# Local attention: the reciprocal of the denominators inside the queries' rotation, and the value products in another order

## The chip, the cores and the metric

The kernel runs on one core of a Trainium2 chip. The metric is the device time of one execution in microseconds (us); the median of three runs is given. TensorE (PE in the profile) does the matmuls and transposes, VectorE (DVE) and ScalarE (ACT) the elementwise work and what is read out of PSUM, GpSimd (POOL) elementwise work between SBUF tensors, and SyncE (SP) issues the transfers.

## The reference, cut to what matters

The whole is a macaron block: half of a two-layer local-attention network, a global attention, and half of the same local-attention network again, over x of 4 x 1024 tokens with 128 channels. The change touches only the local attention, which therefore runs four times (two passes of two layers). Per layer:

```python
q = l2norm(q) * qs;  k = l2norm(k) * ksc          # 8 heads of 64
q, k = rotary_xpos(q, k)                           # x * cos + rotate_half(x) * sin
sim = einsum('bhwid,bhwjd->bhwij', bq, bk)         # 64 queries see their own and the previous block of 64 keys
sim = where((i < j) | (i > j + WINDOW) | (j == -1), -max, sim)
attn = softmax(sim, axis=-1)
out = einsum('bhwij,bhwjd->bhwid', attn, bv)
x = x + out @ wo
```

The softmax is done in pieces: the maximum, the exponentials with their sum (the denominator), one reciprocal of eight sums per row, and a multiplication by it.

## The kernel before, in words

A layer has 32 tiles of 128 tokens. `local_attention_pass` writes the program of each engine out by hand, in order: a `body(i, k)` for the first 28 tiles of a layer, then a written-out end (`attention_end`) in which the last four tiles are woven with the start of the layer's MLP. There are four such stages, so 112 bodies. Engines wait for each other by counting semaphores only; each engine takes its own list strictly as it is written. In the body of tile k the steps belong to different tiles, up to four ahead:

- **PE**: key projection of tile k+4 (L199); eight transposes of tile k's probabilities (L252, the first four into one PSUM bank, the rest into another); query projection of k+4 (L204); value projection of k+3 (L210); the value products of tile k (L268); the scores of k+2 (L239); eight transposes of k+3's rotated and scaled queries and keys (L221); the output projection of k (L279).
- **VectorE**: sums of squares of k+3 (L382); one half of the transposed probabilities of k out of PSUM (`dve_probsT`, L419); the clipped norm of k+3 in four small steps (`dve_clip_norm`, L389, L391, L394, L398); the rotation of k+4's keys and then of its queries (`dve_rotate`, three multiplications each: L374, L375, L376); the reciprocal of k+1 (`dve_inv`, L414); the masked scores and maxima of k+2 (`dve_max`, L404 and eight times L406); the residual of k (L424).
- **GpSimd**: scale the rotated queries and keys of k+3 by their norms (`gp_rotary_scale`, L294, waits for `norm_ready` from L398); multiply the probabilities of k+1 by the reciprocals (`gp_normalise`, L301, waits for `inv_done` from L414); add the two parts of the rotation of k+4 (`gp_rotary_sum`, L288, waits for `q_rotated` from the queries' L376).
- **ScalarE**: exponentials of k+1, slots 2 and 3 (L333); the logarithm and inverse root for the norm of k+3 (L322, L325); the other half of the transposed probabilities (L354); squares of k+4's queries (L308); exponentials of k+1, slots 4 to 7, after which `exp_done` is signalled; copies of the values (L318) and heads (L359); squares of the keys (L313); the first exponential of k+2, the copies of transposed queries and keys (L341, L349, and every fourth tile L348), the second exponential.

`dve_inv` waits for `exp_done` of its tile and for `probs_ready` of two tiles before. The value products of a tile are 16 matmuls in the text: four pairs of heads, two heads of a pair (e), two windows. Head e of a pair uses output partitions 64e to 64e+63, so one half of the columns of the array; window 0 reads `v_first`, window 1 reads `v_second`. The last of the 16 is preceded by the waits of the next scores (`pe_await_scores`).

Of the kernel before, what the change touches and what calls it, by code (L numbers as in the profile page):

```python
# [19 lines left out]
TILE = 128  # L20
# [4 lines left out]
HEADS, DH = 8, 64  # L25
# [20 lines left out]
def tile_of(i, k):  # L46

    return i + k // BATCH_TILES, k % BATCH_TILES
# [93 lines left out]
def local_attention_pass(nc, C, K, W, probs, probsT, z_in, z_out, x, first):  # L142
# [3 lines left out]
    with ExitStack() as ctx:  # L146
        def sb(name, shape, dt=F32):
            return ctx.enter_context(nc.sbuf_tensor(C.own(name), shape, dt))
# [14 lines left out]
        v_second = sb("v_second", [P, 4, INNER])  # L163
        v_first = sb("v_first", [P, 4, INNER])
# [10 lines left out]
        ps = ctx.enter_context(nc.psum_tensor(C.own("ps_attn"), [P, 8, 512], F32))  # L175
        QB, KB, VB, SB0, B5, B6, OB = 0, 1, 2, 3, 5, 6, 7

        def waiting(eng):
            def wait(name, i, k, lag=0, per=1, less=0):

                eng.wait_ge(C[name], i * (BATCH_TILES * per) + (C.at[name] + per * (k + 1 - lag) - less))
            return wait
# [6 lines left out]
        def wait_values(eng, i, k):  # L189

            name = f"v_in{k % 4}"
            eng.wait_ge(C[name], i * 64 + (C.at[name] + 32 * (k // 4 + 1)))
# [33 lines left out]
        def pe_await_scores(pe, wait, i, k):  # L226
            wait("qT_ready", i, k)
            wait("kT_ready", i, k)
            wait("max_done", i, k, 1, HEADS)
# [25 lines left out]
        def pe_values(pe, wait, i, k, scores_next):  # L255
            wait("p5_read", i, k)
            wait("p6_read", i, k)
            wait_values(pe, i, k)
            wait("heads_ready", i, k, 1)
            for pair in range(4):  # L260
                for e in range(2):
                    cols = slice((2 * pair + e) * DH, (2 * pair + e + 1) * DH)
                    out = ps[64 * e:64 * e + 64, OB, pair * TILE:(pair + 1) * TILE]
                    for window, v in ((0, v_first), (1, v_second)):
                        if scores_next and (pair, e, window) == (3, 1, 1):
                            pe_await_scores(pe, wait, *tile_of(i, k + 2))
                        queries = slice(WINDOW * window, WINDOW * (window + 1))
                        last = nc.tensor.matmul(out[:, queries], v[:, k % 4, cols], probsT[:, 4 * e + pair, queries], start=True,  # L268
                                                stop=True, skip_group_check=True)
            last.then_inc(C["av_done"], 1)  # L270
# [88 lines left out]
            nc.scalar.copy(oT[:, :, :], ps[:, OB, :].rearrange("p (a t) -> p a t", t=TILE)).then_inc(C["heads_ready"], 1)  # L359


        def dve_rotate(dve, wait, which, i, k):

            if which:
                wait("k_done", i, k)
                wait("qk_ready", i, k, 2)
            else:
                wait("q_squared", i, k)
            h0 = which * HEADS
            x = ps[:, QB + which, :].rearrange("p (h d) -> p h d", d=DH)  # L370
            table = W["rotary"][:, i // B, k, :, :]
            cos = table[:, which, :].unsqueeze(1).to_broadcast([P, HEADS, DH])
            sin = table[:, 2 + which, :].unsqueeze(1).to_broadcast([P, HEADS, DH])
            nc.vector.tensor_tensor(rot_a[:, k % 2, h0:h0 + HEADS, :], x, cos, ALU.mult)  # L374
            nc.vector.tensor_tensor(rot_b[:, k % 2, h0:h0 + HEADS, 0:32], x[:, :, 32:64], sin[:, :, 0:32], ALU.mult)  # L375
            nc.vector.tensor_tensor(rot_b[:, k % 2, h0:h0 + HEADS, 32:64], x[:, :, 0:32], sin[:, :, 32:64], ALU.mult  # L376
                                    ).then_inc(C["k_rotated" if which else "q_rotated"], 1)

        def dve_ssq(dve, wait, i, k):
            wait("k_squared", i, k)  # L380
            wait("norm_log", i, k, 2)
            nc.vector.reduce_sum(ssq[:, k % 2, :], sq[:, :].rearrange("p (h d) -> p h d", d=DH), AX_X  # L382
                                 ).then_inc(C["ssq_done"], 1)

        def dve_clip_norm(dve, wait, i, k):

            r, n = inorm[:, k % 2, :], newton[:, k % 2, :]
            wait("norm_inv", i, k)
            nc.vector.tensor_tensor(n, r, r, ALU.mult).then_inc(C["newton"], 1)  # L389
            wait("newton", i, k, 0, 2, 1)  # L390
            nc.vector.scalar_tensor_tensor(out=n, in0=n, scalar=-0.5, in1=ssq[:, k % 2, :], op0=ALU.mult, op1=ALU.mult  # L391
                                           ).then_inc(C["newton"], 1)
            wait("newton", i, k, 0, 2)
            nc.vector.scalar_tensor_tensor(out=n, in0=n, scalar=1.5, in1=r, op0=ALU.add, op1=ALU.mult  # L394
                                           ).then_inc(C["newton_done"], 1)
            wait("newton_done", i, k)
            wait("qk_ready", i, k, 2)
            nc.vector.tensor_scalar(cnorm[:, k % 2, :], n, NORM_MOST, None, ALU.min).then_inc(C["norm_ready"], 1)  # L398

        def dve_max(dve, wait, i, k):  # L400
            wait("p6_turned", i, k, 2)
            wait("exp_done", i, k, 2)
            wait("scores_done", i, k)
            nc.vector.memset(slack[:, :], 0.0)  # L404
            for slot in range(HEADS):
                nc.vector.tensor_tensor_reduce(probs[:, k % 2, slot, :],  # L406
                                               ps[:, SB0 + slot // 4, (slot % 4) * SPAN:(slot % 4 + 1) * SPAN],
                                               K["masks"][:, 0 if k == 0 else 1, :], -1.0, MOST, ALU.add, ALU.min,
                                               negmax[:, k % 2, slot:slot + 1]).then_inc(C["max_done"], 1)

        def dve_inv(dve, wait, i, k):
            wait("exp_done", i, k)
            wait("probs_ready", i, k, 2)
            nc.vector.reciprocal(iden[:, k % 2, :], den[:, k % 2, :]).then_inc(C["inv_done"], 1)  # L414

        def dve_probsT(dve, wait, i, k):
            wait("p6_turned", i, k)
            wait("av_done", i, k, 1)
            nc.vector.tensor_copy(probsT[:, 4:8, :], ps[:, B6, :].rearrange("p (a t) -> p a t", t=TILE)).then_inc(C["p6_read"], 1)  # L419

        def dve_residual(dve, wait, i, k):
            wait("wo_done", i, k)
            c = tile_column(i % B, k)
            nc.vector.tensor_tensor(z_out[:, bass.ds(c, TILE)], ps[:, VB, 0:TILE], z_in[:, bass.ds(c, TILE)], ALU.add  # L424
                                    ).then_inc(C["z_done"], 1)
# [232 lines left out]
        def ahead(i, k, n):  # L658

            return 0 <= BATCH_TILES * (i % B) + k + n < TILES  # L660
# [5 lines left out]
        def _(pe):  # L666
# [23 lines left out]
            def attention_end(layer):  # L690
                pe_centre(pe, wait, layer, 0)
                pe_transpose_probs(pe, wait, *t(layer, 28), True)
                pe_project_values(pe, wait, *t(layer, 31))
                pe_values(pe, wait, *t(layer, 28), True)
                pe_scores(pe, *t(layer, 30))
                pe_transpose_qk(pe, wait, *t(layer, 31))
# [4 lines left out]
                pe_transpose_probs(pe, wait, *t(layer, 29), True)  # L701
                pe_var(pe, wait, layer, 1)
                pe_values(pe, wait, *t(layer, 29), True)
                pe_scores(pe, *t(layer, 31))
                pe_centre(pe, wait, layer, 2)
# [372 lines left out]
        def _(dve):  # L1078
            wait = waiting(dve)
            nc.vector.memset(kT[:, :, 0:WINDOW], 0.0).then_inc(C["pass_set"], 1)  # L1080

            def body(i, k):
                if ahead(i, k, 3):
                    dve_ssq(dve, wait, *tile_of(i, k + 3))
                if ahead(i, k, 0):
                    dve_probsT(dve, wait, i, k)
                if ahead(i, k, 3):
                    dve_clip_norm(dve, wait, *tile_of(i, k + 3))
                if ahead(i, k, 4):
                    dve_rotate(dve, wait, 1, *tile_of(i, k + 4))  # L1090
                    dve_rotate(dve, wait, 0, *tile_of(i, k + 4))
                if ahead(i, k, 1):
                    dve_inv(dve, wait, *tile_of(i, k + 1))
                if ahead(i, k, 2):
                    dve_max(dve, wait, *tile_of(i, k + 2))
                if ahead(i, k, 0):
                    dve_residual(dve, wait, i, k)
# [67 lines left out]
            for tile in range(WOVEN):  # L1165
                body(*t(0, tile))
# [40 lines left out]
            for tile in range(WOVEN):  # L1207
                body(*t(1, tile))
# [1582 lines left out]
```

## Time and profile before

| | |
|---|---|
| median of the runs | 1967.95 us (1967.82 to 1968.98) |
| the profiled execution | 1970.34 us, span 1968.4 us |
| busy share of the span | PE 96%, DVE 84%, ACT 76%, POOL 47% |
| one body in the steady part of a stage | 7.58 us |

A line of the profile names the engine, the line of the kernel, the operation, output and input, how many, how long, and, in brackets, how long the engine was idle before and what ended that. PEld is TensorE's loading of weights, which runs beside its matmuls. The ends of matmuls are modelled and consecutive ones overlap, so TensorE's pace is read from where its instructions start. The share of PE is of the whole program; the change sits in the four stages of local attention.

### The profile page before, as it was taken

The numbers are of one execution on the slowest core, as the hardware profiler recorded it, in microseconds if no ns is written. First come the engines' busy times: TensorE is split into PE (matmuls) and PEld (weight loads), VectorE is DVE, ScalarE is ACT, GpSimd is POOL, SyncE is SP. The second block draws the span as 40 slices with busy tenths as digits, with TensorE's granted clock in tenths as the row PEclk, the third lists the DMA queues.
The fourth block names the chain that finished last, engine by engine and source line by source line (L and its number), as shares of the span: only waits on it lengthen the run. The fifth ranks groups of instructions, "written<-read, shape, count | busy, mean of one in ns | idle before, by whom it ended". The sixth has DMA issues, their size and how long they took to land. (4 is left out here: it accounts for less than half of the span.)

```text
span 1968.4 us, 61233 instructions
## 1 busy us (share of the span) xinstructions
PE 1891.7 (96%) x22590; PEld 1117.6 (57%) x22590; DVE 1649.2 (84%) x5474; ACT 1502.9 (76%) x4121; POOL 915.5 (47%) x548
## 2 busy tenths in 40 slices
PE   7999999999999989999999998899999999999998
PEld 3777763577775343443443367436777645777753
DVE  6899975899995678999999769769999659999955
ACT  5899994799997353777777754469999848999963
POOL 2778760488882040000000046338887406888800
PEclk9999999999999986999999999999999999999999
DMA  6112120112121040111111000002222201121201
GB/s 188 44 44 48 44 67 6 33 45 49 44 66 23 6 154 27 41 41 42 42 42 42 20 5 2 2 20 49 45 47 45 58 6 42 43 49 44 67 16 43
DMA packets 76138, 85.63 MB, mean 44 GB/s; under 512 B 17135, under 2 KB 50499, under 8 KB 75715
## 3 DMA queue, kind: packets, MB, share of 16 engines
q1 hardware_dynamic: 75647, 81.70, 16.5%
q8 instruction: 182, 2.98, 0.6%
q14 instruction: 113, 0.93, 0.1%
q10 hardware_dynamic: 196, 0.02, 0.0%
HBM read 21.16 MB, written 8.39 MB: 15 GB/s over the span
## 5 line engine op out<-in xcount | busy, mean ns | idle before, releaser
L333 ACT ACTIVATE probs<-probs,negmax 128x128 f32<-128x128 f32 x1024 | 399.9, 396 | 24.8 <-DVE negmax L406 24.3
L2168 ACT ACTIVATE gprobs<-ps_global 128x1024 f32<-128x1024 f32 (+3 forms) x384 | 291.5, 811 | 125.6 <-PE ps_global L1633 102.9
L288 POOL TENSOR_TENSOR rot<-rot 128x1024 f32<-128x1024 f32 x128 | 302.1, 2361 | 144.7 <-DVE rot L376 144.7
L294 POOL TENSOR_TENSOR qk<-rot,cnorm 128x1024 f32<-128x1024 f32 x128 | 243.7, 1904 | 122.1 <-POOL rot L288 92.1
L301 POOL TENSOR_TENSOR probs<-probs,iden 128x1024 f32<-128x1024 f32 x128 | 242.8, 1897 | 119.5 <-DVE iden L414 119.5
L1863 DVE TENSOR_REDUCE maxes<-ps_global 128x1 f32<-128x512 f32 (+2 forms) x384 | 222.0, 638 | 11.4 <-PE ps_global L1596 6.5
L406 DVE CUSTOM_DVE_ANT_0 probs<-ps_attn,masks 128x128 f32<-128x128 f32 x1024 | 225.5, 283 | 0.0
L1591 PE MATMUL ps_global<-kq 48*128 48x512 bf16 (+3 forms) x768 | 197.3, 346 | 7.0 <-DVE maxes L1863 1.8
L333 ACT ACTIVATION_READ_ACCUMULATOR probs<-probs,negmax 128x1 f32 x1024 | 197.3, 193 | 0.0
L374 DVE TENSOR_TENSOR rot<-ps_attn,rotary 128x512 f32<-128x512 f32 x256 | 174.9, 683 | 2.1 <-PE ps_attn L199 1.6
L2098 POOL CAST m_parts<-m_turn 32x128 bf16<-32x128 f32 x16 | 4.5, 279 | 364.5 <-DVE m_turn L1877 364.5
L268 PEld LDWEIGHTS ps_attn<-probsT,v_first 128*64 128x64 f32 x2048 | 118.1, 136 | 98.1 <-ACT probsT L354 94.3
L1648 PE MATMUL ps_global<-gprobs,v_all 128*9 128x512 f32 (+3 forms) x1536 | 161.1, 491 | 1.7 <-ACT gprobs L2168 1.7
L252 PEld LDWEIGHTS ps_attn<-ident,probs 128*128 128x128 f32 x1024 | 118.5, 141 | 69.4 <-POOL probs L301 63.1
L221 PE MATMUL ps_attn<-ident,qk 128*128 128x128 f32 x1024 | 140.6, 281 | 15.4 <-POOL qk L294 4.7
L633 ACT ACTIVATE ln<-ps_attn,vecs_sb 128x512 f32<-128x512 f32 (+2 forms) x96 | 65.6, 683 | 116.8 <-PE ps_attn L595 72.7
L382 DVE TENSOR_REDUCE ssq<-sq 128x16 f32<-128x1024 f32 x128 | 154.5, 1207 | 0.1
L1859 DVE CUSTOM_DVE_ANT_0 ps_global<-ps_global,later 128x384 f32<-128x384 f32 (+1 forms) x256 | 152.1, 652 | 2.7 <-PE ps_global L1591 0.8
L1591 PEld LDWEIGHTS ps_global<-kq 48*128 48x128 bf16 x768 | 58.8, 94 | 160.5 <-DVE maxes L1863 86.7
L1624 PE MATMUL ps_global<-kq 51*128 51x512 bf16 (+3 forms) x768 | 145.7, 329 | 2.2 <-ACT gprobs L2168 1.9
L268 PE MATMUL ps_attn<-probsT,v_first 128*64 128x64 f32 x2048 | 138.5, 230 | 0.7 <-ACT probsT L354 0.7
L221 PEld LDWEIGHTS ps_attn<-ident,qk 128*128 128x128 f32 x1024 | 110.4, 141 | 45.1 <-POOL qk L294 38.5
(220 smaller groups left out, 4608.6 us busy)
## 6 DMA issues: line engine op xcount, KB each, us to landing
v_first<-v_second SPq DMA_DIRECT2D x256, 128.0 KB, 2.3
hs<-z_a SPq DMA_DIRECT2D x256, 32.0 KB, 1.9
ln<-z_b SPq DMA_DIRECT2D x56, 128.0 KB, 2.4
kq<-split_scratch SPq DMA_DIRECT2D x64, 96.0 KB
kq<-split_scratch SPq DMA_DIRECT2D x64, 64.0 KB
split_scratch<-parts SPq DMA_DIRECT2D x8, 384.0 KB, 4.1
split_scratch<-gprobs SPq DMA_DIRECT2D x6, 384.0 KB, 4.1
x_tok<-in_x_dram SPq DMA_DIRECT2D x4, 512.0 KB, 6.0
```

The lines of the kernel that those rows point to most:

```text
L221: last = nc.tensor.transpose(ps[:, b, pair * TILE:(pair + 1) * TILE], qk[:, k % 2, which * INNER + pair * 128:which * INNER + (pair + 1) * ...
L268: last = nc.tensor.matmul(out[:, queries], v[:, k % 4, cols], probsT[:, 4 * e + pair, queries], start=True, stop=True, skip_group_check=True)
L288: nc.gpsimd.tensor_tensor(a, a, b, ALU.add).then_inc(C["rot_sum"], 1)
L294: nc.gpsimd.tensor_tensor(qk[:, k % 2, :].rearrange("p (h d) -> p h d", d=DH), rot_a[:, k % 2, :, :], cnorm[:, k % 2, :].unsqueeze(2).to_b ...
L301: nc.gpsimd.tensor_tensor(pr, pr, iden[:, k % 2, :].unsqueeze(2).to_broadcast([P, HEADS, SPAN]), ALU.mult).then_inc(C["probs_ready"], 1)
L333: last = nc.scalar.activation(probs[:, k % 2, slot, :], probs[:, k % 2, slot, :], ACT.Exp, scale=-1.0, bias=negmax[:, k % 2, slot:slot + 1 ...
L374: nc.vector.tensor_tensor(rot_a[:, k % 2, h0:h0 + HEADS, :], x, cos, ALU.mult)
L406: nc.vector.tensor_tensor_reduce(probs[:, k % 2, slot, :], ps[:, SB0 + slot // 4, (slot % 4) * SPAN:(slot % 4 + 1) * SPAN], K["masks"][:, ...
L1591: mm = nc.tensor.matmul(out, qs[buf][rows, p, tile_cols(t)], ks[buf][rows, p, CHUNK * c:CHUNK * c + w], start=True, stop=not masked_here, ...
L1648: mm = nc.tensor.matmul(ps[32 * h:32 * h + AD + 1, O0, t0 - CHUNK * c:CHUNK], v_all[:, S_TILES * (n // GROUPS) + s, GROUP * (n % GROUPS) + ...
L1863: nc.vector.reduce_max(maxes[:, n % 2, r, p0:p1, t, c], ps[:, bank_of(use), 0:len(both) * w].rearrange("q (p s) -> q p s", s=w), AX_X).the ...
L2168: nc.scalar.activation(probs[:, step % RING, 2 * p:2 * p + 2, 0:w], ps[:, S0 + 2 * p:S0 + 2 * p + 2, 0:w], ACT.Exp).then_inc(C["p2_exp"], 1)
```

## The change

Two edits. In the body, the reciprocal of tile k+1 is issued by VectorE after the first of the three multiplications of the queries' rotation of tile k+4, instead of after the third. All bodies have a tile k+4, so the `elif` is for none of them; the ends of a stage and the first tiles before it call `dve_rotate` and `dve_inv` as before. And the 16 value products of a tile are written pair, window, head instead of pair, head, window, so that the two heads of a pair come in turn; the wait for the next scores stays ahead of the last of the 16.

```diff
             for pair in range(4):
-                for e in range(2):
-                    cols = slice((2 * pair + e) * DH, (2 * pair + e + 1) * DH)
-                    out = ps[64 * e:64 * e + 64, OB, pair * TILE:(pair + 1) * TILE]
-                    for window, v in ((0, v_first), (1, v_second)):
-                        if scores_next and (pair, e, window) == (3, 1, 1):
+                for window, v in ((0, v_first), (1, v_second)):
+                    for e in range(2):
+                        cols = slice((2 * pair + e) * DH, (2 * pair + e + 1) * DH)
+                        out = ps[64 * e:64 * e + 64, OB, pair * TILE:(pair + 1) * TILE]
+                        if scores_next and (pair, window, e) == (3, 1, 1):
...
-        def dve_rotate(dve, wait, which, i, k):
+        def dve_rotate(dve, wait, which, i, k, inv_of=None):
...
             nc.vector.tensor_tensor(rot_a[:, k % 2, h0:h0 + HEADS, :], x, cos, ALU.mult)
+            if inv_of is not None:
+                dve_inv(dve, wait, *inv_of)
             nc.vector.tensor_tensor(rot_b[:, k % 2, h0:h0 + HEADS, 0:32], x[:, :, 32:64], sin[:, :, 0:32], ALU.mult)
...
                     dve_rotate(dve, wait, 1, *tile_of(i, k + 4))
-                    dve_rotate(dve, wait, 0, *tile_of(i, k + 4))
-                if ahead(i, k, 1):
+                    dve_rotate(dve, wait, 0, *tile_of(i, k + 4), tile_of(i, k + 1))
+                elif ahead(i, k, 1):
                     dve_inv(dve, wait, *tile_of(i, k + 1))
```

## Rows read from the trace of the kernel before

**Rows 1.** Busy time by stretches; one attention stage. The first line names the columns.
```profile
core 0: us, PE busy (x) PEld busy (x) DVE busy (x) ACT busy (x) POOL busy (x), PEclk, DMA share, GB/s
376.00:590.00 214.00, 211.76 (x3591) 153.48 (x3569) 205.71 (x882) 204.25 (x716) 172.41 (x86) 1.00 0.23 52
```

**Rows 2.** Who waited for whom, 376.7 to 588.94: us in total, times, longest.
```profile
PEld ps_attn L252 <- POOL probs L301: 15.0, 28, 0.5
...
PEld ps_attn L221 <- POOL qk L294: 8.0, 27, 0.3
ACT probs L333 <- DVE negmax L406: 5.9, 26, 0.3
DVE probsT L419 <- PE ps_attn L252: 5.4, 27, 0.2
```

**Rows 3.** Timeline of PE in one steady body: start us, duration us, engine, line, operation.
```profile
499.47 1.02 PE L199 MATMUL ps_attn<-wqkv_sb,hs 128*128 128x512 f32 x2
...
504.14 1.00 PE L239 MATMUL ps_attn<-kT,qT 64*32 64x96 f32 x64
...
505.22 0.86 PEld L221 LDWEIGHTS ps_attn<-ident,qk 128*128 128x128 f32 x8 [0.30 <-POOL qk L294]
...
507.05 1.02 PE L199 MATMUL ps_attn<-wqkv_sb,hs 128*128 128x512 f32 x2
...
507.91 1.04 PE L252 MATMUL ps_attn<-ident,probs 128*128 128x128 f32 x8
```

**Rows 4.** Timeline of PE at the start of the second stage.
```profile
378.38 1.02 PE L199 MATMUL ps_attn<-wqkv_sb,hs 128*128 128x512 f32 x2
...
383.05 1.00 PE L239 MATMUL ps_attn<-kT,qT 64*32 64x96 f32 x64
383.98 1.09 PE L221 MATMUL ps_attn<-ident,qk 128*128 128x128 f32 x8
...
385.80 1.02 PE L199 MATMUL ps_attn<-wqkv_sb,hs 128*128 128x512 f32 x2
```

**Rows 5.** Timeline of DVE in the same steady body.
```profile
501.40 0.69 DVE L419 COPY probsT<-ps_attn 128x512 f32<-128x512 f32 x1 [0.19 <-PE ps_attn L252]
502.01 0.50 DVE L389 TENSOR_TENSOR newton<-inorm 128x16 f32<-128x16 f32 x1
...
502.96 0.17 DVE L398 TENSOR_SCALAR cnorm<-newton 128x16 f32<-128x16 f32 x1
...
504.90 0.41 DVE L375 TENSOR_TENSOR rot<-ps_attn,rotary 128x256 f32<-128x256 f32 x1
...
505.57 0.19 DVE L414 RECIPROCAL iden<-den 128x8 f32<-128x8 f32 x1
505.69 0.28 DVE L406 CUSTOM_DVE_ANT_0 probs<-ps_attn,masks 128x128 f32<-128x128 f32 x1
```

**Rows 6.** Timeline of POOL and the last exponential's end on ACT, same body.
```profile
500.11 2.36 POOL L288 TENSOR_TENSOR rot<-rot 128x1024 f32<-128x1024 f32 x1
...
503.27 1.90 POOL L294 TENSOR_TENSOR qk<-rot,cnorm 128x1024 f32<-128x1024 f32 x1 [0.79 <-POOL rot L288]
...
504.20 0.19 ACT L333 ACTIVATION_READ_ACCUMULATOR probs<-probs,negmax 128x1 f32 x1
...
505.83 1.90 POOL L301 TENSOR_TENSOR probs<-probs,iden 128x1024 f32<-128x1024 f32 x1 [0.67 <-DVE iden L414]
```

**Rows 7.** Timeline of DVE at the start of the second stage.
```profile
381.05 0.18 DVE L389 TENSOR_TENSOR newton<-inorm 128x16 f32<-128x16 f32 x1
```

**Rows 8.** Costliest groups of the whole page: one of the value products' two.
```profile
L268 PE MATMUL ps_attn<-probsT,v_first 128*64 128x64 f32 x2048 | 138.5, 230 | 0.7 <-ACT probsT L354 0.7
```

**Rows 9.** Timeline of PE: the value products of one steady body.
```profile
503.01 0.34 PE L268 MATMUL ps_attn<-probsT,v_first 128*64 128x64 f32 x4
...
503.18 0.29 PE L268 MATMUL ps_attn<-probsT,v_second 128*64 128x64 f32 x4
...
503.30 0.33 PE L268 MATMUL ps_attn<-probsT,v_first 128*64 128x64 f32 x4
...
503.41 0.33 PE L268 MATMUL ps_attn<-probsT,v_second 128*64 128x64 f32 x4
```

## The prediction

> **What bounds the kernel now.** The page's shares come first: TensorE is busy for 96% of the span. That is an average over unlike stages, so the next view is the one by stretches. In an attention stage of 214 us TensorE is busy 211.76, VectorE 205.71, ScalarE 204.25, GpSimd 172.41 [rows 1]: three engines near full, so what counts is which wait really holds TensorE. The view of waits of one stage offers two from GpSimd [rows 2]: the transposes of the probabilities (L252) on L301, 15.0 us, and the transposes of queries and keys (L221) on L294, 8.0 us. The timeline tells them apart. A body takes 7.58 us (L199 at 499.47 and at 507.05). L252's first matmul starts at 507.91, 0.86 after L199's; the key projection's two passes alone need that long (1.02 with the modelled tail), so this wait only delays a weight load beneath a running matmul and costs nothing [rows 3]. L221 differs. Its load starts at 505.22, 1.08 after the scores L239 began at 504.14 [rows 3]; at the start of the second stage L221 follows L239 by 0.93 (383.05 to 383.98), without a wait, and from one L199 to the next there are 7.42 us (378.38 to 385.80) [rows 4]. So TensorE's own work is 7.42 us a body, and in the steady part it loses about 0.16 ahead of L221, in every body.
>
> Why is L294 late? It starts at 503.27, 0.14 after the end of L398 (502.96 and 0.17), the last step of the norm, although GpSimd has been idle for 0.79 [rows 5, 6]; the row names the older L288 as releaser, but that had ended. The norm's first step, L389, is 16 columns wide and takes 0.50; at the start of the stage the same instruction took 0.18 [rows 5, 7]. It ends at 502.51, and GpSimd's L288 ran from 500.11 to 502.47 [rows 5, 6]: L389 is held until L288 is done. L288 comes after L301 on GpSimd, L301 waits for the reciprocal L414 (505.57, then L301 at 505.83) [rows 5, 6]. So a late reciprocal makes L301 late, that L288, that L389, that L294, and that TensorE's L221. VectorE has just 0.19 idle per body, ahead of L419 [rows 2, 5].
>
> **The change, part by part.**
>
> *The reciprocal.* It takes the place of L375: 504.90 instead of 505.57, 0.67 earlier [rows 5]. The work is the same, one instruction of 0.19, and no instruction is added. L301 follows a reciprocal by 0.26, so it could start at 505.16; L294 ends at 505.17, so GpSimd goes straight on at about 505.2 instead of 505.83 [rows 6], some 0.6 earlier, and L288 behind it ends near 501.85 instead of 502.47 in the frame of the rows. That is ahead of L389's 502.01: L389 takes 0.18 and not 0.50. L398 then ends at 502.81, L294 starts at 502.95 and ends at 504.85, 0.32 earlier than now. L221 could start 0.05 later, at 504.90; TensorE cannot before 504.14 + 0.93 = 505.07. So the whole stall goes, with 0.17 in hand. Worth: 7.58 - 7.42 = 0.16 in each of the 112 bodies except the first two of a stage, which run at 7.42 already: 104 x 0.16 = 16.6 us.
>
> *What the move passes.* It goes ahead of two multiplications, so `q_rotated` (for L288, and for the next query projection) comes 0.13 later than without it (L414 to L406 start 505.57 to 505.69); L288 no longer waits for that but for L301, so it is hidden. The added risk is the wait for `exp_done` in front of L375: behind it are L375, L376, the eight maxima and the residual. The last exponential's sum is read at 504.20 + 0.19 = 504.39 [rows 6]; VectorE would now be at the reciprocal at 504.90 - 0.32 = 504.58. ScalarE's exponentials follow the query projection, which follows L252, as does L419; so they keep this distance, about 0.2. If it shrinks, VectorE has an idle 0.19 + 0.32 - 0.16 = 0.35 per body ahead of L419 to pay from. Past this point TensorE is itself the last to be ready. ScalarE's busy time is 204.25/214 x 7.58 = 7.23 a body, VectorE's 7.29 - 0.32 = 6.97 [rows 1].
>
> *The order of the value products.* 2048 records over 128 tiles are 16 a tile for one window: eight matmuls, each in two passes [rows 8]. The first four of `v_first` start within the 0.34 from 503.01, before any of `v_second` at 503.18 [rows 9]. In the text only two of these four (first head) stand ahead of `v_second`; so the heads, in different halves of the columns, already run side by side. The first `v_second` group of four takes 0.29, that of the second pair 0.33 [rows 9]: at the second pair the second head falls 0.04 behind, since its work stands behind four passes of the first head. In turn, its work is next in line, and I expect all groups at 0.29. The gain lies between 0 (the halves already overlap) and 0.04 a tile (they start together, as in the first pair); a loss would need the halves to stop overlapping, against which the rows speak, as the first pair runs in turn already. I take 0.04, the row of the first pair being the same situation: 112 x 0.04 = 4.5 us. This counts only because the stall at L221 goes: L221's release leaves 0.17, of which 0.04 is used. Alone, it would only lengthen that stall.
>
> The page "TensorE: Matmul & The Clock Gate" of the Trainium skill, section "The mechanism", gives TensorE a "64-deep reorder window" that pulls weight loads ahead of matmuls in flight; a tile's 16 products with their loads would all lie in it, any order would be the same, and the sum would be 16.6 alone. By the same section matmuls start in program order; the four `v_first` ahead of `v_second` disagree with that [rows 9].
>
> *Sum.* 16.6 + 4.5 = 21.1 us. The profiled execution is 1970.34, so 1949.2; the median of the runs shown lies 2.4 below it: 1946.9, say 1947.
>
> **The rivals.**
>
> 1. *The order of the products changes nothing*: the 0.04 is not in the order but in something else, such as the next pair's loads. Only the reciprocal acts: 1967.95 - 16.6 = 1951.4. For it: the halves already overlap. Against: the first pair's 0.29. This is where the rule above leads as well. Chance 0.2.
> 2. *ScalarE becomes the bound.* It waits 5.9/28 = 0.21 a body for the first maximum [rows 2]. If this wait stays, 7.23 + 0.21 = 7.44 is its pace, and a copy that only every fourth tile has makes it uneven, for which I put 0.04 by choice: 7.48, a gain of 0.10 x 112 = 11 us, 1957. Against: the maxima come 0.32 earlier in the frame of L419 (VectorE's earlier norm), which covers the wait. Chance 0.12.
> 3. *The change does not do what it says*: L389 is slow for another reason than L288, or L301 is not released earlier. Then L221 keeps its stall and TensorE its 7.58: 1968. Against: L389's end 0.04 after L288's, and 0.18 without it. Chance 0.05.
> 4. *Slower: the reciprocal now waits for the exponentials* and holds the rotation, the maxima and the sums of squares behind it. VectorE's pace is 6.97 plus that wait plus some 0.10 between instructions (7.58 - 0.19 - 7.29), so it passes the present 7.58 when the wait is over 0.51, that is, if `exp_done` came after 505.1 in the frame of the rows, 0.7 later than now. With a wait of 0.68 it would cost 0.17 x 112 = 19 us: 1987. Against: `exp_done` is there at 504.39 and follows TensorE's query projection, which the change does not delay. Chance 0.05.
>
> **How the numbers follow.** The forecast, both parts acting, has 0.58: 1947. Its own spread: the four ends of stages may gain up to 0.32 each and 16 more tiles 0.04 each, 1.9 in all, down to 1945; a small wait left could take 2 off the gain. The first rival reaches to about 1953; that makes 0.78, and about half of the second lies below it. So 1943 to 1953. A measurement can tell about 0.2%, 4 us, from no change. Faster by more than that: the forecast, the first rival and nearly all of the second, 0.58 + 0.2 + 0.10 = 0.88; within: 0.07; slower: 0.05.
>
> **What would show it.** Right: a body of 7.38 to 7.39 in the steady part; L221's load about 0.15 after the last of L239's, without the name of L294; L389 at 0.17 to 0.18 throughout; L301 directly behind L294; L414 at the old place of L375 without a wait; VectorE idle for about 0.3 ahead of L419; all `v_second` groups of four at 0.29. Wrong in the second part: groups still at 0.33, a body of 7.42. Wrong in the first: L389 still at 0.50, or a wait of L414 for the exponentials of over 0.3, or ScalarE still waiting 0.2 for L406 with a body between 7.42 and 7.58.

## The result, and the profile after

The changed kernel takes 1945.1 us (median of four runs, 1943.69 to 1945.89); the kernel before, 1967.91 on the same chip. The ratio is 0.9882, 95% interval 0.9865 to 0.9899: 22.8 us faster, where the forecast of 1947 had said about 21. The profiled execution went from 1970.34 to 1945.89 us, its span from 1968.4 to 1944.0.

The same attention stage as in [rows 1], after (same columns). The stage now ends sooner, so the stretch is taken shorter, to lie within it:

```profile
376.00:575.00 199.00, 198.57 (x3380) 144.97 (x3370) 187.33 (x836) 193.81 (x679) 164.66 (x82) 1.00 0.22 50
```

TensorE's busy share of the stretch goes from 99.0% (211.76 of 214) to 99.8% (198.57 of 199). VectorE's busy time for one body falls from 7.29 us (205.71/214 x 7.58) to 6.95 (187.33/199 x 7.38), 0.34 less for the same work: the norm's first step alone takes 0.33 less (0.50 to 0.17), so what is gone is time in which an instruction was held and counted as busy. Who waited for whom in the second stage, 376.7 to 575, which is 27 bodies where [rows 2] has 28:

```profile
PEld ps_attn L252 <- issue: 14.2, 54, 0.3
...
DVE probsT L421 <- PE ps_attn L252: 8.0, 26, 0.3
...
ACT probs L333 <- DVE negmax L408: 0.2, 1, 0.2
PEld ps_attn L221 <- POOL qk L294: 0.2, 1, 0.2
```

The wait of the transposes L221 for GpSimd's L294 is down from 27 times to one, ScalarE's for the first maximum from 26 to one, and VectorE's for the transposed probabilities has grown from 5.4 to 8.0 us, from 0.19 to 0.30 a body: VectorE gets there earlier than before. One steady body, answering to [rows 3, 5, 6, 9] (new line numbers: L421 was L419, L391 was L389, L400 was L398, L416 was L414, L408 was L406):

```profile
496.52 2.37 POOL L288 TENSOR_TENSOR rot<-rot 128x1024 f32<-128x1024 f32 x1
...
496.67 1.02 PE L199 MATMUL ps_attn<-wqkv_sb,hs 128*128 128x512 f32 x2
...
497.53 1.04 PE L252 MATMUL ps_attn<-ident,probs 128*128 128x128 f32 x8
...
498.60 0.69 DVE L421 COPY probsT<-ps_attn 128x512 f32<-128x512 f32 x1 [0.32 <-PE ps_attn L252]
...
499.21 0.17 DVE L391 TENSOR_TENSOR newton<-inorm 128x16 f32<-128x16 f32 x1
...
499.83 0.17 DVE L400 TENSOR_SCALAR cnorm<-newton 128x16 f32<-128x16 f32 x1
...
500.13 1.91 POOL L294 TENSOR_TENSOR qk<-rot,cnorm 128x1024 f32<-128x1024 f32 x1 [1.24 <-issue]
...
500.38 0.29 PE L268 MATMUL ps_attn<-probsT,v_second 128*64 128x64 f32 x4
...
500.61 0.29 PE L268 MATMUL ps_attn<-probsT,v_second 128*64 128x64 f32 x4
...
501.30 1.00 PE L239 MATMUL ps_attn<-kT,qT 64*32 64x96 f32 x64
501.40 0.19 ACT L333 ACTIVATION_READ_ACCUMULATOR probs<-probs,negmax 128x1 f32 x1
...
501.78 0.19 DVE L416 RECIPROCAL iden<-den 128x8 f32<-128x8 f32 x1
...
502.05 1.90 POOL L301 TENSOR_TENSOR probs<-probs,iden 128x1024 f32<-128x1024 f32 x1
...
502.22 0.86 PEld L221 LDWEIGHTS ps_attn<-ident,qk 128*128 128x128 f32 x8
...
504.04 1.02 PE L199 MATMUL ps_attn<-wqkv_sb,hs 128*128 128x512 f32 x2
```

From L199 to L199 there are 7.37 us to the rounding of the rows. L288 ends at 498.89, 0.32 before the norm's first step L391, which takes 0.17. L301 follows L294 at once (502.04 to 502.05). L221 follows L239 by 0.92. The reciprocal comes 0.19 after the last exponential is read out, without a wait.

### The profile page after: what moved, and what is told of

It reads as the page before. It is cut to its first block and busy times, and to the rows that moved or that the text cites. A ratio compares the mean times of both kernels' runs of the same rounds, so it can differ in the third digit from the quotient of the medians.

```text
span 1944.0 us, 61233 instructions
## 1 busy us (share of the span) xinstructions
PE 1876.9 (97%) x22590; PEld 1112.2 (57%) x22590; DVE 1614.2 (83%) x5474; ACT 1501.3 (77%) x4121; POOL 916.5 (47%) x548
## 5 line engine op out<-in xcount | busy, mean ns | idle before, releaser
L288 POOL TENSOR_TENSOR rot<-rot 128x1024 f32<-128x1024 f32 x128 | 302.6, 2364 | 144.2 <-DVE rot L378 144.2
L294 POOL TENSOR_TENSOR qk<-rot,cnorm 128x1024 f32<-128x1024 f32 x128 | 244.0, 1906 | 170.5 <-issue 146.8
L301 POOL TENSOR_TENSOR probs<-probs,iden 128x1024 f32<-128x1024 f32 x128 | 242.9, 1898 | 45.7 <-DVE iden L416 44.9
L408 DVE CUSTOM_DVE_ANT_0 probs<-ps_attn,masks 128x128 f32<-128x128 f32 x1024 | 226.4, 286 | 0.7 <-issue 0.5
L333 ACT ACTIVATION_READ_ACCUMULATOR probs<-probs,negmax 128x1 f32 x1024 | 204.2, 199 | 0.0
L268 PEld LDWEIGHTS ps_attn<-probsT,v_first 128*64 128x64 f32 x2048 | 103.7, 137 | 97.7 <-ACT probsT L354 93.9
L252 PEld LDWEIGHTS ps_attn<-ident,probs 128*128 128x128 f32 x1024 | 119.8, 141 | 66.9 <-issue 64.2
L221 PE MATMUL ps_attn<-ident,qk 128*128 128x128 f32 x1024 | 140.8, 281 | 6.0 <-POOL qk L294 3.7
L279 PE MATMUL ps_attn<-oT,wo_sb 128*128 128x128 f32 x1024 | 135.2, 275 | 0.0
L252 PE MATMUL ps_attn<-ident,probs 128*128 128x128 f32 x1024 | 132.8, 273 | 0.6 <-POOL probs L301 0.6
```

The source lines that it names most:

```text
L252: last = nc.tensor.transpose(ps[:, b, s * TILE:(s + 1) * TILE], probs[:, k % 2, 4 * e + s, :], K["ident"][:, :])
L288: nc.gpsimd.tensor_tensor(a, a, b, ALU.add).then_inc(C["rot_sum"], 1)
L294: nc.gpsimd.tensor_tensor(qk[:, k % 2, :].rearrange("p (h d) -> p h d", d=DH), rot_a[:, k % 2, :, :], cnorm[:, k % 2, :].unsqueeze(2).to_b ...
L301: nc.gpsimd.tensor_tensor(pr, pr, iden[:, k % 2, :].unsqueeze(2).to_broadcast([P, HEADS, SPAN]), ALU.mult).then_inc(C["probs_ready"], 1)
L333: last = nc.scalar.activation(probs[:, k % 2, slot, :], probs[:, k % 2, slot, :], ACT.Exp, scale=-1.0, bias=negmax[:, k % 2, slot:slot + 1 ...
L408: nc.vector.tensor_tensor_reduce(probs[:, k % 2, slot, :], ps[:, SB0 + slot // 4, (slot % 4) * SPAN:(slot % 4 + 1) * SPAN], K["masks"][:, ...
```

## The experiments

Ratios are to the kernel before on the same chip.

| edit | median us | ratio, 95% interval |
|---|---|---|
| reciprocal only | 1950.55 | 0.9905 (0.989 to 0.992) |
| order of the products only | 1968.61 | 0.9995 (0.9986 to 1.0004) |
| both, reciprocal one multiplication later | 1944.07 | 0.9871 (0.9857 to 0.9884) |
| both, an addition behind L288 | 2004.8 | 1.0177 (1.0163 to 1.0191) |
| both, a fill of 128x512 behind L288 | 1944.55 | 0.9877 (0.9863 to 0.9892) |
| both, a fill of 128x1024 behind L288 | 1946.66 | 0.9885 (0.9871 to 0.99) |
| reciprocal, products in blocks of two pairs | 1993.33 | 1.0124 (1.0109 to 1.0139) |
| reciprocal, products in blocks of four pairs | 2040.12 | 1.0358 (1.034 to 1.0375) |
| both, output projection of three pairs (leaves out the fourth) | 1923.53 | 0.9766 (0.975 to 0.9783) |

**The reciprocal alone.** The changed kernel with the loops of the value products as before:

```diff
-                for window, v in ((0, v_first), (1, v_second)):
-                    for e in range(2):
+                for e in range(2):
...
+                    for window, v in ((0, v_first), (1, v_second)):
```

> The reciprocal moved as in the change, the value products in the old order. If the two parts are worth what I gave them (the stall ahead of L221 goes, and the products' halves keep their lag), a body takes 7.42 to 7.43 us and the time is about 1950.5 us. If the order of the products is worth nothing, it is the changed kernel's 1945. If the order had to be changed for the stall to go, it is 1968.

It came to 1950.55. Timeline of TensorE and its loads in one body:

```profile
501.19 0.34 PE L268 MATMUL ps_attn<-probsT,v_second 128*64 128x64 f32 x4
...
501.93 1.00 PE L239 MATMUL ps_attn<-kT,qT 64*32 64x96 f32 x64
502.85 1.09 PE L221 MATMUL ps_attn<-ident,qk 128*128 128x128 f32 x8
504.68 1.02 PE L199 MATMUL ps_attn<-wqkv_sb,hs 128*128 128x512 f32 x2
...
512.10 1.02 PE L199 MATMUL ps_attn<-wqkv_sb,hs 128*128 128x512 f32 x2
```

7.42 us a body, L221 0.92 behind L239, and the products' groups still 0.34 wide. So the stall goes by the reciprocal alone, and the lag of the second heads stays.

**The order alone.** The kernel before with the new loops (the diff's first hunk).

> The value products in the new order, the reciprocal in its old place. My theory: the products take about 0.048 us less per tile, and the stall ahead of L221 grows by the same 0.048, to about 0.20, because its release (L294 behind the held L389) does not hang on the products: a body stays at 7.58 and the time at 1968. The rival, that each part saves its own share of TensorE's time whatever the other does: 112 x 0.048 = 5.4 us less, 1962.5.

```profile
502.77 0.29 PE L268 MATMUL ps_attn<-probsT,v_second 128*64 128x64 f32 x4
...
503.00 0.29 PE L268 MATMUL ps_attn<-probsT,v_second 128*64 128x64 f32 x4
...
506.63 1.02 PE L199 MATMUL ps_attn<-wqkv_sb,hs 128*128 128x512 f32 x2
...
514.22 1.02 PE L199 MATMUL ps_attn<-wqkv_sb,hs 128*128 128x512 f32 x2
```

The products did get shorter (0.29 for the second pair's group too), the body stayed at 7.59 by the rows, and the loads say where it went:

```profile
503.69 0.78 PEld L239 LDWEIGHTS ps_attn<-kT,qT 64*32 64x32 f32 x64
...
504.81 0.85 PEld L221 LDWEIGHTS ps_attn<-ident,qk 128*128 128x128 f32 x8 [0.34 <-POOL qk L294]
```

L221 comes 1.12 behind L239, where it was 1.08 [rows 3]: 0.04 of TensorE's work became 0.04 of waiting. The interval, 0.9986 to 1.0004, leaves no room for the rival's 5.4 us.

**The reciprocal one multiplication later.** Does every delay of the reciprocal cost, or only one that makes L288 run into the norm?

```diff
-            if inv_of is not None:
-                dve_inv(dve, wait, *inv_of)
             nc.vector.tensor_tensor(rot_b[:, k % 2, h0:h0 + HEADS, 0:32], x[:, :, 32:64], sin[:, :, 0:32], ALU.mult)
+            if inv_of is not None:
+                dve_inv(dve, wait, *inv_of)
```

> As the changed kernel, but the reciprocal after the second of the three multiplications, 0.33 us later. By the changed kernel's rows L301 would then start at 502.38 instead of 502.05 and L288 end near 506.6, just where the norm's first step starts (506.59); L294 has 0.18 in hand before L221. So my theory, in which only a held norm step makes L221 late, expects no change: 1945, L301 idle for about 0.3 ahead of it. A theory in which every delay of L301 is passed on, as by a GpSimd that bounds the body, expects up to 0.33 x 112 = 37 us more.

GpSimd in one body:

```profile
499.76 2.36 POOL L288 TENSOR_TENSOR rot<-rot 128x1024 f32<-128x1024 f32 x1
503.04 1.91 POOL L294 TENSOR_TENSOR qk<-rot,cnorm 128x1024 f32<-128x1024 f32 x1 [0.92 <-POOL rot L288]
505.28 1.90 POOL L301 TENSOR_TENSOR probs<-probs,iden 128x1024 f32<-128x1024 f32 x1 [0.34 <-DVE iden L416]
```

L301 is 0.34 late, and L288 ends at 502.12, at the very start of the norm's first step, which still takes 0.17:

```profile
502.12 0.17 DVE L391 TENSOR_TENSOR newton<-inorm 128x16 f32<-128x16 f32 x1
```

The time is that of the changed kernel within the intervals. So of the 0.67 by which the change moves the reciprocal, the first half was enough.

**What holds the norm's first step.** The changed kernel with one more operation on GpSimd behind `gp_rotary_sum` in the body, on a tile of its own: an addition, or a fill of 512 or of 1024 columns. Shown is the addition; the fill has `nc.gpsimd.memset(spare[:, :], 0.0)` in its place.

```diff
                 if ahead(i, k, 4):
                     gp_rotary_sum(gp, wait, *tile_of(i, k + 4))
+                    gp_spare(gp)
...
+            nc.gpsimd.tensor_tensor(spare[:, :], K["centre"][:, 0:1].to_broadcast([P, 512]), K["centre"][:, 0:1].to_broadcast([P, 512]), ALU.add).then_inc(C["spare_done"], 1)
```

> As the changed kernel, with one more addition of 128x512 on GpSimd behind L288 in each body, which reads SBUF and writes a tile that nobody reads; about 0.95 us by half of the 1.90 of a 128x1024 row. GpSimd has 1.24 idle there. My theory (the norm's first step is held while such an operation of GpSimd runs): from reciprocal to reciprocal 0.27 + 1.85 + 2.37 + 0.95 + 0.04 + 0.45 + 1.95 = 7.88 us, over the 7.38 of TensorE, so a body of about 7.88 and 1945 + 112 x 0.50 = 2001 us, with the first step at about 0.6 to 0.8 us. The rival (the first step is slow for a reason of VectorE's or ScalarE's own): GpSimd's idle time takes the addition, 1945.

> As the changed kernel, with a fill of 128x512 on GpSimd behind L288 in each body, which writes a tile that nobody reads and reads nothing. Its duration is not in the trace; I expect 0.4 to 0.95 us. If any operation of GpSimd holds the norm's first step, that step is held to the end of the fill, and a body grows to 6.93 us plus the fill, if that is over 7.38: 1945 to 2001. If only one that reads SBUF does, nothing is held: 1945. The Trainium skill's page SBUF - State Buffer, section Who interferes with whom, says that a VectorE instruction with two SBUF inputs contends with a GpSimd instruction that reads SBUF, and not with one that only writes it; by it this run is at 1945 and the run with the addition is not.

> As the run with the fill, but 128x1024, so about 1.05 us by twice the 0.53 of the fill of 128x512, which ended so near to the norm's first step that a hold would have been some 0.02 us only. This one begins about 0.35 us ahead of that step and ends some 0.5 after it. If a GpSimd operation that only writes holds the step too, the step takes 0.6 to 0.8 us and the body about 7.9, as with the addition: near 2000. If only one that reads does, the step stays at 0.17 and the time at 1945.

The addition, GpSimd and then VectorE (here L304 is the scaling, L298 the sum, L186 the addition, L394 the sums of squares, L401 the norm's first step, L410 its last, L231 the transposes of queries and keys):

```profile
499.48 1.90 POOL L304 TENSOR_TENSOR qk<-rot,cnorm 128x1024 f32<-128x1024 f32 x1 [0.79 <-issue]
...
503.24 2.36 POOL L298 TENSOR_TENSOR rot<-rot 128x1024 f32<-128x1024 f32 x1
505.56 1.04 POOL L186 TENSOR_TENSOR spare<-centre 128x512 f32<-128x512 f32 x1
507.39 1.90 POOL L304 TENSOR_TENSOR qk<-rot,cnorm 128x1024 f32<-128x1024 f32 x1 [0.79 <-issue]
```

```profile
503.75 1.21 DVE L394 TENSOR_REDUCE ssq<-sq 128x16 f32<-128x1024 f32 x1
...
505.80 0.83 DVE L401 TENSOR_TENSOR newton<-inorm 128x16 f32<-128x16 f32 x1
...
507.08 0.17 DVE L410 TENSOR_SCALAR cnorm<-newton 128x16 f32<-128x16 f32 x1
```

The step starts at 505.80 and ends at 506.63, 0.03 after the addition's 506.60. GpSimd still idles for 0.79 before L304, so it is not short of time; the scaling is late because the norm is: it starts 0.14 after the end of L410 (507.25). The wait of the transposes of queries and keys is back, and the body takes 7.91 us (L304 at 499.48 and 507.39), against 7.88 worked out before:

```profile
PEld ps_attn L231 <- POOL qk L304: 16.0, 24, 0.7
```

2004.8 instead of 1945.1 is 59.7 us for 112 additions, though they lie in idle time of an engine. Not every VectorE step is held: the sums of squares L394 read one input from SBUF, run wholly beside the sum L298, and take their 1.21 us; in the kernel before the two overlap in 124 of the 128 tiles, and none of the 128 took more than 1.22. The fill of 1024 columns covers the step from end to end, and the step keeps its 0.17 (GpSimd, then VectorE):

```profile
506.96 0.94 POOL L186 MEMSET spare<- 128x1024 f32 x1
```

```profile
507.33 0.17 DVE L401 TENSOR_TENSOR newton<-inorm 128x16 f32<-128x16 f32 x1
```

Over all 128 tiles the step's median is 0.165 us with this fill and 0.834 with the addition. So it is not GpSimd's being at work that holds the step: the two operations that read SBUF, the sum and the addition, held it, and the one that only writes did not. This agrees with the sentence on two SBUF inputs that the expectation takes from the Trainium skill's page "SBUF — State Buffer", section "Who interferes with whom". The shorter fill ended too near to the step to tell, as its successor's expectation says; its 1944.55 agrees.

**How far TensorE looks for the other half.** The products of the changed kernel in blocks, all first heads of a block and then its second heads (the edit for blocks of four):

```diff
-            for pair in range(4):
-                for window, v in ((0, v_first), (1, v_second)):
-                    for e in range(2):
+            for block_of in range(4 // 4):
+              for e in range(2):
+                for pair in range(4 * block_of, 4 * block_of + 4):
...
+                    for window, v in ((0, v_first), (1, v_second)):
```

> As the changed kernel, but the value products in blocks: two pairs of the first heads (eight passes), then the same two pairs of the second heads, and so for the other two pairs. If the halves run side by side whatever stands between them in the program, the products of a tile stay at 0.93 to 0.98 us from first to last start and the time at 1945 to 1951. If TensorE starts the second half only when it is among the next few passes, the halves overlap in part: with nothing overlapped the products would take 32 x 0.058 = 1.87 us, so up to 0.94 more a body and 1945 + 105 = 2050; I expect something between, 1955 to 2030.

> As the changed kernel, but all four pairs of the first heads (16 passes) and then all four of the second heads. If the order does not matter, 1945 to 1951. If TensorE starts the second half only when it is near in the program, hardly anything overlaps: up to 0.94 more a body, near 2050, and more than with blocks of two pairs.

Blocks of four pairs, TensorE (L269 are the products here):

```profile
500.13 1.00 PE L239 MATMUL ps_attn<-kT,qT 64*32 64x96 f32 x64
506.43 0.33 PE L269 MATMUL ps_attn<-probsT,v_first 128*64 128x64 f32 x2
506.59 0.28 PE L269 MATMUL ps_attn<-probsT,v_second 128*64 128x64 f32 x2
...
507.06 0.28 PE L269 MATMUL ps_attn<-probsT,v_second 128*64 128x64 f32 x2
507.17 0.34 PE L269 MATMUL ps_attn<-probsT,v_first 128*64 128x64 f32 x4
507.29 0.33 PE L269 MATMUL ps_attn<-probsT,v_second 128*64 128x64 f32 x4
507.46 0.28 PE L269 MATMUL ps_attn<-probsT,v_first 128*64 128x64 f32 x2
...
508.25 1.00 PE L239 MATMUL ps_attn<-kT,qT 64*32 64x96 f32 x64
```

Groups of two are one half alone, groups of four are both. Twelve of the first heads' 16 passes run alone; the second heads start with the thirteenth (507.17), which is when four passes of the first half are left. Then the second heads go on alone. With blocks of two pairs the same is seen on a smaller scale, four of the first heads' eight passes alone:

```profile
503.25 0.33 PE L269 MATMUL ps_attn<-probsT,v_first 128*64 128x64 f32 x2
503.42 0.28 PE L269 MATMUL ps_attn<-probsT,v_second 128*64 128x64 f32 x2
503.53 0.34 PE L269 MATMUL ps_attn<-probsT,v_first 128*64 128x64 f32 x4
```

The cost over the changed kernel is 48.2 us for the blocks of two and 95.0 for those of four, or 0.38 and 0.74 for each of the 128 tiles; nothing overlapped at all had been put at 0.94. In these two cases TensorE takes up the second half when four passes of the first, with their loads, are ahead of it, not from anywhere in the tile. The old order has four passes between: there the first pair of heads began together and the next ones lost 0.04. That this lag comes from the same limit is argued from these runs, not shown by itself.

**What bounds it now.** The changed kernel with a smaller output projection:

```diff
-            for pair in range(4):
+            for pair in range(3):
...
-                                        start=(pair == 0), stop=(pair == 3))
+                                        start=(pair == 0), stop=(pair == 2))
```

> As the changed kernel, but the output projection sums three of the four pairs of heads and leaves out the last, two matmul passes or 0.22 us of TensorE a tile. If TensorE now sets the body with 7.38 us, the body falls to 7.16, or to ScalarE's busy 7.19 with a little more if that is then the bound: 1945 - 112 x 0.2 = 1921 to 1931. If something else sets the body (GpSimd's chain, the maxima, a transfer), it stays at 7.38 and the time at 1945.

1923.53, so 21.6 us less, 0.19 a body of the 0.22 left out. One body of TensorE, the stretch view of the second stage in the columns of [rows 1], and a wait in it:

```profile
497.61 1.02 PE L199 MATMUL ps_attn<-wqkv_sb,hs 128*128 128x512 f32 x2
...
504.76 1.02 PE L199 MATMUL ps_attn<-wqkv_sb,hs 128*128 128x512 f32 x2
```

```profile
376.00:570.00 194.00, 192.54 (x3342) 139.05 (x3341) 187.87 (x838) 191.41 (x679) 164.48 (x82) 1.00 0.23 52
```

```profile
PEld ps_attn L221 <- POOL qk L294: 2.9, 8, 1.0
```

TensorE did set the body: 72 of the 108 steps from one body to the next take 7.15 or 7.16 us, the whole 0.22 less. The others are longer, most of them by less than 0.1. The second stage has eight waits of L221 for L294 again, and ScalarE is then busy for 191.41 of 194 us, 98.7%. In a body of 7.38 (L199 at 461.59 and 468.97) ScalarE's part of the norm came late and the wait was 0.37; what makes each of the others longer was not followed up. Among the runs that leave nothing out, none beats the changed kernel; the later reciprocal is equal to it within the intervals.

## Why the prediction was right

- *L252's wait costs nothing, L221's costs 0.16 a body.* Right. With the reciprocal alone the body is 7.42 and L221 follows L239 by 0.92; in the changed kernel the loads of L252 still idle 14.2 us, where it was 15.0, now without the name of L301, and L252's first matmul still follows L199's by 0.86 (496.67 to 497.53): it costs nothing.
- *The chain from the reciprocal over L301, L288 and the held norm step to L294 and L221.* Right. Moving the reciprocal halfway already frees the step and the stall is gone; an addition of 1.04 us in GpSimd's idle time holds the step again (0.83) and brings the stall back.
- *The size of the first part*, 16.6 us. By the rows 7.58 to 7.42; against the kernel before on its chip the run with the reciprocal alone is 19.1 us faster (ratio 0.9905, so 15.8 to 21.7 of 1969.6), which holds the 16.6. In its profiled execution the 108 steps from one body to the next, L199 to L199, are together 16.2 us shorter than before.
- *The order*, 0.04 a tile from the width of the groups: 7.42 to 7.37 or 7.38 by the rows, slightly more. The term was small by about 0.01, because the rows of the groups show the lag to two digits only and the halves now also start closer together than the first pair did (0.007 us apart by the trace's single records, there 0.014); over 112 bodies that is 1.1 us. The run with the reciprocal alone and the changed kernel differ by 5.4 us, where 4.5 had been said. *Alone it would only lengthen the stall*: right, shown by the run of the order alone.
- *The sum*, 21.1, against 22.8 by the medians and 24.4 by the two profiled executions. The starts of L199 in the two timelines divide the gain: of the 108 steps from one body to the next, 97 are shorter by 0.17 to 0.22 and six by 0.07 or less, 21.6 together; the last body of each stage with what follows it, up to the next stage or the end, is shorter by 0.58 to 0.65, 2.4 for the four. So 104 bodies for the first part was close, though in the second stage only the first body ran at 7.42 before and the second already took 7.55 (L199 at 378.38, 385.80 and 393.35). What the sum left out is the ends of the stages, which the prediction had in its spread alone.
- *The wait for the exponentials* (the slower rival): the reciprocal comes 0.19 after them, where 0.2 was said, and does not wait. *ScalarE as the bound*: its wait for the first maximum is gone, as was argued from the earlier norm; with 0.22 less on TensorE it is nearly full and delays single bodies, not most. *The order changes nothing*: wrong, as 7.42 to 7.38 shows, and the blocks show that it can matter by up to 0.74 a tile, with 12 passes of each half alone in the blocks of four. That any order would be the same was the prediction's own reading of the "64-deep reorder window" of the Trainium skill's page "TensorE: Matmul & The Clock Gate", section "The mechanism"; the section says of the window only that weight loads are pulled ahead of matmuls in flight, and the blocks of four disagree with the reading.
- *VectorE's idle time ahead of the transposed probabilities*: about 0.3 was said, 0.32 stands in the row.

## What to carry to other kernels

Look for the short instruction with a long duration: a 16-column step of 0.50 us beside the same step at 0.17 was what made the stall, and the releasers named by the profile pointed to its neighbours. Follow a wait round the loop before you price an edit: the order of the products was worth nothing alone and 0.05 us a body once the other wait was gone. Idle time on GpSimd isn't free for work that reads SBUF when VectorE has a step with two SBUF inputs on the critical chain, and here matmuls for the two halves of the array's columns did best next to each other in the program.

## What the runs showed of the hardware that I had not expected

The reach with which TensorE finds work for the idle half of its columns is short: four passes with their weight loads, in blocks of 8 and of 16 passes alike, so two sequences of 16 passes overlapped by four only. And a fill on GpSimd of 0.94 us over the whole of VectorE's 0.17 us step did not disturb it, where an addition of 1.04 us in the same place held it, so that it took 0.83.
